# Moving the maxima, the placing and the value copy inside the two attention stages of a fused twelve-stage kernel

## What is computed

```python
# kind 0: 16 heads of 4 x 512 positions, 8 features a head; q, k and v are the same
qh = q.reshape(HEADS, b, s, hd)
scores = jnp.einsum('hbqd,hbkd->hbqk', qh, kh) * scale
attn = jax.nn.softmax(scores, axis=-1)
out = jnp.einsum('hbqk,hbkd->hbqd', attn, vh)
# kind 3: keys in blocks of 128, a maximum for each block
s_blk = jnp.einsum('bhqd,bhkd->bhqk', q, k_blk) * scale
m = jnp.max(s_blk, axis=-1, keepdims=True)
e = jnp.exp(s_blk - m)
num = num + jnp.einsum('bhqk,bhkd->bhqd', e, v_blk)
den = den + jnp.sum(e, axis=-1, keepdims=True)
```

## Time and profile before

| | us |
|---|---|
| median of three runs | 1760.11 |
| the profiled execution | 1750.36 |
| its span, first to last instruction | 1748.5 |
| TensorE busy in the span | 1552.6 (89%) |
| VectorE busy | 1225.0 (70%) |
| ScalarE busy | 1022.8 (58%) |
| GpSimd busy | 587.8 (34%) |
| exponentials (L2594), 512 instructions | 273.1 |
| maxima (L2657), 512 instructions | 320.6 |

### The profile page before, as it was taken

How to read it: one execution, slowest core, us unless ns; L and a number is a source line. 1 busy time by engine, 2 the same in 40 slices (tenths; PEclk the granted TensorE clock), 3 DMA queues, 4 the chain that set the end, 5 groups by cost and what they waited for, 6 DMA issues and landing times.

```text
span 1748.5 us, 25287 instructions
## 1 busy us (share of the span) xinstructions
PE 1552.6 (89%) x9032; PEld 1051.4 (60%) x9032; DVE 1225.0 (70%) x2811; ACT 1022.8 (58%) x1826; POOL 587.8 (34%) x734
## 2 busy tenths in 40 slices
PE   6998799998999799859999987997796799998896
PEld 4776323333677588637888965897695422222695
DVE  6788688994788733473535967596786688884785
ACT  4554488886554455335537733774374388877374
POOL 1775311111377100123006633663534211111432
PEclk9999899999999999979999989999998899999898
DMA  3211634300221400010000000000553643300464
GB/s 117 66 57 32 126 39 55 55 1 1 83 81 33 157 8 1 0 37 13 1 1 12 1 1 1 2 1 1 178 187 122 155 72 55 55 1 1 162 197 145
DMA packets 68116, 101.05 MB, mean 58 GB/s; under 512 B 17584, under 2 KB 53720, under 8 KB 67129
## 3 DMA queue, kind: packets, MB, share of 16 engines
q1 hardware_dynamic: 65047, 93.39, 20.9%
q0 software_dynamic: 2944, 6.05, 1.0%
HBM read 87.60 MB, written 15.78 MB: 59 GB/s over the span
## 4 chain that ended last, share of the span: by engine, by line
PE 26%; DVE 15%; ACT 8%; POOL 4%; issue 3%; DMA 2%; SPq 0%; POOLq 0%; DVEq 0%; ACTq 0%
PE bank L97 6%; PE bank L99 5%; PE bank L98 5%; DVE x L1571 5%; ACT e L2594 4%; POOL sorted L2084 2%; DVE hl L2052 2%; ACT qq L2577 2%; DVE mx L2657 2%; PE bank L2495 1%; PE bank L190 1%; PE bank L2480 1%; DVE hh L2050 1%; PE bank L2448 1%; PE bank L194 1%
## 5 line engine op out<-in xcount | busy, mean ns | idle before, releaser
L2657 DVE TENSOR_REDUCE mx<-bank 128x1 f32<-128x512 f32 (+1 forms) x512 | 320.6, 681 | 56.2 <-PE bank L2448 55.2
L2594 ACT ACTIVATE e<-bank 128x512 f32<-128x512 f32 x512 | 273.1, 600 | 50.7 <-PE bank L2480 47.7
L2480 PE MATMUL bank<-qq,kk 99*128 99x512 bf16 (+1 forms) x512 | 163.6, 384 | 14.2 <-ACT e L2594 13.7
L1587 POOL TENSOR_TENSOR midl<-mid,midh 128x512 fp32r<-128x512 f32 (+1 forms) x96 | 126.0, 1319 | 77.1 <-ACT midh L1507 77.0
L2480 PEld LDWEIGHTS bank<-qq,kk 99*128 99x128 bf16 (+1 forms) x512 | 38.7, 97 | 163.0 <-ACT e L2594 125.5
L1090 DVE TENSOR_TENSOR hl<-q,hh 128x512 fp32r<-128x512 f32 x64 | 44.9, 701 | 127.1 <-ACT hh L1060 105.2
L97 PE MATMUL bank<-wdh,midh 128*128 128x256 f32 (+1 forms) x384 | 112.9, 294 | 9.7 <-DVE x L1571 9.7
L99 PE MATMUL bank<-wdh,midl 128*128 128x256 f32 (+1 forms) x384 | 110.4, 288 | 0.0
L98 PE MATMUL bank<-wdl,midh 128*128 128x256 f32 (+1 forms) x384 | 110.2, 287 | 0.0
L228 POOL TENSOR_SCALAR rs<-mv 128x4 f32<-128x4 f32 x48 | 11.4, 237 | 285.1 <-DVE mv L215 284.2
L1502 ACT ACTIVATE mid<-bank,bu 128x512 f32<-128x512 f32 (+1 forms) x96 | 65.9, 686 | 62.4 <-PE bank L99 55.2
(11 more groups left out here) (401 smaller groups left out, 4414.7 us busy)
## 6 DMA issues: line engine op xcount, KB each, us to landing
w<-in_expert_w SPq DMA_DIRECT2D x30, 963.0 KB, 5.3
qq<-scratch SPq DMA_DIRECT2D x18, 384.0 KB
w<-in_L_ffn_w_kernel SPq DMA_DIRECT2D x16, 344.0 KB
w<-in_L_ffn_w_kernel SPq DMA_DIRECT2D x16, 320.0 KB
wo<-in_L_ffn_wo_kernel SPq DMA_DIRECT2D x16, 320.0 KB, 3.0
scratch<-e SPq DMA_DIRECT2D x34, 128.0 KB, 4.7
sorted<-in_unsorted SPq DMA_DIRECT2D x2, 1935.0 KB, 11.3
g<-sorted SPq DMA_DIRECT2D x30, 129.0 KB, 2.3
```

Source lines behind the costliest of these rows:

```text
L1587: e.tensor_tensor(l[0:fn, o], mid[i % 2][0:fn, o], h[0:fn, o].bitcast(F32), ALU.subtract).then_inc(*l2_m_lo.tick(n, i, f))
L2480: e.matmul(b_bank(t, u, j), keys(kk[0:K], t, b)[:, k * 128:(k + 1) * 128], queries(qq[0:K], t, b), start=True, stop=True).then_inc(*at_b.t ...
L2594: e.activation(er[u][:, j * 512:(j + 1) * 512], b_bank(t, u, j), ACT.Exp, bias=0.0, scale=scale).then_inc(*at_e.tick(n, t, u, j))
L2657: e.tensor_reduce(mxa[t % 3][:, o:o + nkb], bank[place_a["a", t, u, j]].rearrange("p (k n) -> p k n", k=nkb), X, ALU.max).then_inc(*at_max ...
```

## The change

`AHEAD` goes from 15 to 12. In the main loop the placing of the next head goes from u = 2 to u = 5; its four spreadings go from u = 2, 3, 4, 5 to u = 5, 6, 7, 7; the values of the next head go from u = 6 to u = 3. The prologue is shorter by three units, and its placing, spreading and reordering of keys sit at other units. The work itself is the same.

```diff
-            AHEAD = 15
+            AHEAD = 12
...
-                if i == 8:
+                if i == 9:
                     order.append(("place", 0, 0))
-                if 8 <= i < 12:
-                    order.append(("spread", 0, i - 8))
-                if kind == 0 and i in (5, 11, 14):
-                    order.append(("keys", 0, {5: 1, 11: 2, 14: 3}[i]))
+                if i in (9, 10, 11):
+                    order.append(("spread", 0, i - 9))
+                if i == 11:
+                    order.append(("spread", 0, 3))
+                if kind == 0 and i in (5, 8, 11):
+                    order.append(("keys", 0, {5: 1, 8: 2, 11: 3}[i]))
...
-                if u == 2 and t + 1 < 16:
+                if u == 5 and t + 1 < 16:
                     order.append(("place", t + 1, 0))
-                if 2 <= u < 6 and t + 1 < 16:
-                    order.append(("spread", t + 1, u - 2))
+                if u >= 5 and t + 1 < 16:
+                    order.append(("spread", t + 1, u - 5))
+                if u == 7 and t + 1 < 16:
+                    order.append(("spread", t + 1, 3))
...
-                if u == 6 and t + 1 < 16 and kind == 0:
+                if u == 3 and t + 1 < 16 and kind == 0:
                     order.append(("values", t + 1, 0))
```

## The result

The changed kernel takes 1785.77 us (median of four runs, 1783.09 to 1791.8) where the kernel before takes 1759.7: a ratio of 1.015, with an interval of 1.0125 to 1.0175. It is slower by 26 us; 20 were forecast, and 1785.8 lies in the range of 1760 to 1792.

A forecast was written before the change was run, and what follows sets the result against it. The prediction took a placing-to-placing loop closed by the split's latency as the bound. Heads of 13.63 and 13.38 us, with starts and other heads, gave +12.0 in kind 3 and +8.2 in kind 0: 1780 us, range 1760 to 1792.

The forecast's parts named there:

- The loop of kind 3: Kind 3's cycle from one placing to the next, closed by the split's latency: forecast 0.78 us longer a head, 13.63.
- P: The placing in the main loop, at u = 5 after the change; starting point from which the forecast counts times.
- E0: First exponential of a head; the next head's was forecast at 5.74 us after the placing in kind 3.
- Cost nothing above the loop: Kind 0's value matmuls at u = 3: TensorE reaches the placing about P + 13.35, just under the split's 13.38.
- The same loop with a split of 16 in place of 64 columns: Kind 0 before the change: heads of 12.60 us set by kind 3's loop, with a split 0.25 us shorter.
- The start of kind 0: Shorter prologue of kind 0: first exponential at 209.8, a gain of 5.4 us, and first placing at 216.7.
- The start of kind 3: Stores hold kind 3's first exponential at 1401.55, so no gain; first placing 7.14 us later, at 1408.7.
- Other heads: Extra time of non-plain heads between first and last placing: 3.3 us in kind 3, 11.6 in kind 0.
- from there the code is the same: After head 15's first exponential in kind 3 no further cost was counted, leaving that kind at +12.0 us.
- that rival's 12.7: Rival that the split is hidden: TensorE's order bounds heads, 12.7 us in kind 3; total 1764, chance 0.12.
- The b of unit 1: Rival that this matmul needn't wait for the first exponential's bank: heads 12.44 and 12.19, total 1747, chance 0.08.
- The rival of the falling clock: TensorE's waits within heads halve its clock: 9 us more a head, three such heads give 1807; chance 0.04.

The follow-up runs named there:

- the second chip: The changed kernel run again on another chip beside the kernel before: 1775.3 us, ratio 1.0171, 26.5 us above before.

## Why the prediction was right, point by point

In short: the mechanism was right in kind 3, while in kind 0 the size of the heads came out nearly right through a loop that isn't the one that bounds them. That part is luck.

**The loop of kind 3: right at each step.** Forecast and measured, from P: b 1.30 and 1.31; its exponential 1.72 and 1.73; E0 5.74 and 5.76; the four last reductions 8.98 and 9.00; from there to the placing 4.65 and 4.56; the head 13.63 and 13.56. Two experiments take single terms out of it. With the fourth cast gone from in front of E0, 0.60 goes of the 0.60 it was priced at (2.31 less 1.71). With maxima far ahead, the split and its four reductions drop out, and another wait appears 0.35 lower. The kernel at `AHEAD` 13, with a single cast per unit, is back at 12.77. So what made heads longer in kind 3 is the paired casts together with four maxima behind the last released bank.

**The values in kind 0: mis-sized.** The step "Cost nothing above the loop", at about P + 13.35 under a split at 13.38, measured P + 13.55: the values were through at P + 11.50 for 11.4, and the bank wait behind the copy was 0.31 where 0.21 had been put. Two terms 0.03 apart were too close to say which is last. It is 0.17 a head, 2.4 us in all, and the kernel with the values one unit later gives exactly that back.

**Kind 0 before: wrong, without harm to the number.** "The same loop with a split of 16 in place of 64 columns" wasn't what bounded it: a split shorter by a step left its heads at 12.59. The number of before was read off, not rebuilt from kind 0's own rows, and fourteen heads at 12.60 were counted where half of the plain ones take 12.93. The 13.38 for after came out at 13.37 with the values out of the way, but there too the placing doesn't wait for GpSimd by its rows, so that the number fits and the bound isn't shown. Shown for kind 0 are the 0.60 of the paired cast and the 0.18 of the values; what makes up the rest of its 0.95 isn't.

**The start of kind 0: nearly.** First exponential 209.62 for 209.8; first placing 217.81 for 216.7, with the granted clock at half from 211.5 on for 10.2 us. The kernels with the old prologue that ran later (split in four steps, placing at u = 3) have the same 10.2 us there, so that it need not be the change's doing. **The start of kind 3: the mechanism right, a term missing.** The stores held the exponentials back, as forecast. But the first placing came 8.73 us behind E0 and not 7.14: TensorE waited 5.12 us at E0 and then ran at half clock. "Nothing points to it" had looked at the waits within heads, where the clock indeed stayed at 1.00; the wait that the change makes at the start, some 5 us by the forecast's own numbers, hadn't been looked at.

**Other heads: in kind 0 a match by chance.** 12.1 for 11.6 in kind 0, 4.7 for 3.3 in kind 3. Kind 0's 12.1 holds the head of 17.83 with its half clock. On the second chip, without that, the other heads take 8.7.

**The last head: a term missing.** The forecast's "from there the code is the same" priced it at nothing. In kind 0 the exponentials of head 15 run 9.86 us from first to last on both chips, where they ran 8.69 before; the granted clock was half for 3.4 us from 426.6 on. In kind 3 it is 9.81 for 8.64 on the first chip, and 8.64 again on the second.

**The sum.** Kind 0: forecast +8.2; with 2.4 for the values, 1.1 for the first placing and 0.5 for other heads, 12.2; measured at E0 of head 15, 425.39 - 413.13 = 12.3. This only splits up the difference of one profile, and 3.4 of it belong to the one head with the half clock. Kind 3: forecast +12.0; with 1.6 for the start, 1.4 for other heads and 1.0 back on plain heads, 14.0; measured 13.6 from the statistics before the stage to E0 of head 15. To the ends of the stages, last heads included, it is 13.9 + 14.8 = 28.7 on the first chip and 11.5 + 12.4 = 23.9 on the second; the medians say 26. The other 13 us of the first chip's two profiles, which differ by 41, lie in stages that the change doesn't touch. The clock was half for 211.8 us of the one span and 156.4 of the other; how much of the 13 that makes isn't shown.

**The rivals.** The split isn't hidden in kind 3 (the marker on the placing), and where it was hidden, with `AHEAD` at 15, heads took 13.21 and not that rival's 12.7. The b of unit 1 did wait for ScalarE. The rival of the falling clock had a place, and a smaller size than its 9 us a head: the head of 17.83 in kind 0 took 3.4 us more than on the second chip. In the plain heads behind it and in those of kind 3 from 1444.5 on, the clock stayed at 1.00. The Trainium skill's rule (TensorE: Matmul & The Clock Gate, "A second HAM failure mode: psum-queue depth-cycling") isn't seen in these heads, at 1.00 with TensorE busy 12.26 of 13.56 us. The half clock at the starts is another matter.

## What to carry to other kernels

Moving a producer and its consumer together by the same number of units doesn't keep their distance in time: count what each engine has queued between them, and look for what stood in front of the pair and now stands behind it (here an o, and two casts in one unit). Follow the loop from a step to its own next turn by starts of instructions, and trust it as the bound only where the marker on its last step names it; two loops within 0.2 us of each other have to be derived both. And before a load or copy is moved forward, look for the last reader of what it overwrites.

## What wasn't expected of the hardware

At the start of kind 3, TensorE had been at full clock for 17.1 us, since 1402.8, and its clock fell to half in the middle of a single wait of 5.12 us. In the kernel with more filling it fell 0.8 us behind a wait of 2.29 us, and stayed there for 10.2. With the split in four steps the wait at that place was 2.72 us, and the clock fell only 5.8 us behind it, for 3.4 us; in the kernel before, the wait was 1.18 and the clock stayed at 1.00. After waits of 6.40 us (`AHEAD` 15) and 7.41 (fourth cast late) it was half for 13.7 and 17.1 us. So the longer waits came with the longer stretches, but 2.29 cost more than 2.72, and no run here says why. GpSimd's four and five dependent steps on small tiles took 0.3 to 0.45 us each from start to start, and one step less was worth 0.29 us a head in kind 3 and nothing in kind 0.
